# Text rows projected once per table row and spread by one-hot products, in an early-fusion block on one core

## The reference, cut to what matters

```python
# x: (32, 96, 96, 3) images, x_txt: (32, 32) tokens; D = 256, H = 512, S = 16
h = einsum(patchify(x), W_proj) + b_proj + pos_emb           # 36 image rows per sample
t = take(weights, positions(x_txt))                          # 32 text rows per sample
h = concatenate([h, t], axis=1)                              # 68 rows x 32 samples
xn = layernorm(h)
u = xn @ W_x.T + b_x
g = sigmoid(xn @ W_g.T + b_g)
u = u * g + depthwise_conv3(u) * (1 - g)
dt = clip(softplus(xn @ W_dt.T + b_dt).mean(axis=(0, 1)), 0.001, 2.0)   # one per hidden unit
y = ssm_scan(u, exp(A * dt), ...)                            # A = -softplus(A_raw)
h = h + layernorm(xn + y @ W_out.T + b_out)
h = h + moe_top2_of_4(layernorm(h))
```

## Time and profile before

| | us |
|---|---|
| runs (3) | 497.41, 498.78, 499.92 |
| median | 498.78 |
| span of the profiled execution | 495.2 |
| median less span | 3.6 |
| PE busy in the span | 442.5 (89%) |
| DVE busy | 330.5 (67%) |
| ACT busy | 296.4 (60%) |

### The profile page before, as it was taken

One profiled execution on the slowest core, in us unless ns is written; L12 is line 12 of the kernel. 1 busy time (PEld: TensorE's weight loads), 2 busy tenths in 40 slices (PEclk: granted clock), 3 DMA queues, 4 the chain that ended last, 5 costly groups with the idle time before them and its releaser, 6 DMA issues.

```text
span 495.2 us, 9980 instructions
## 1 busy us (share of the span) xinstructions
PE 442.5 (89%) x3149; PEld 363.4 (73%) x3149; DVE 330.5 (67%) x980; ACT 296.4 (60%) x667; POOL 152.2 (31%) x255
## 2 busy tenths in 40 slices
PE   8989989799899999999999798999999999999400
PEld 5769967667778878887777577888878888888300
DVE  6885567678999434335786777866674666666584
ACT  2854359177975465316554354887786777877341
POOL 2000000000000000001243887874778644543322
PEclk9999999799999999999999999999999999999955
DMA  7981089900019942972511222232322333252262
GB/s 178 187 228 56 33 253 322 292 0 2 1 35 259 217 114 58 228 228 81 180 54 52 89 94 77 86 97 66 107 98 76 107 107 110 74 155 69 78 213 82
DMA packets 58734, 59.94 MB, mean 121 GB/s; under 512 B 25368, under 2 KB 51260, under 8 KB 57404
## 3 DMA queue, kind: packets, MB, share of 16 engines
q1 hardware_dynamic: 54236, 48.68, 36.4%
q0 software_dynamic: 3552, 9.74, 5.3%
q10 hardware_dynamic: 896, 0.89, 0.6%
HBM read 34.50 MB, written 24.80 MB: 120 GB/s over the span
## 4 chain that ended last, share of the span: by engine, by line
PE 66%; DVE 12%; issue 7%; ACT 7%; POOL 4%; DMA 2%; SPq 1%; DVEq 0%; POOLq 0%; ACTq 0%
PE bank L1040 14%; PE bank L881 9%; PE bank L433 8%; PE bank L435 8%; PE bank L434 8%; PE bank L955 3%; PE bank L1030 3%; PE bank L901 3%; POOL sorted_x L671 2%; PE bank L1012 2%; ACT U L470 1%; DVE spj L1400 1%; DMA got<-expert_y 1%; PE bank L848 1%; PE bank L947 1%
## 5 line engine op out<-in xcount | busy, mean ns | idle before, releaser
L1040 PE MATMUL bank<-w,hr 128*128 x320 | 76.0, 380 | 1.5 <-DVE ysb L1661 1.5
L1040 PEld LDWEIGHTS bank<-w,hr 128*128 128x128 f32 x320 | 60.1, 190 | 11.7 <-issue 2.7
L644 POOL MEMSET ones<- 2x128 f32 x1 | 0.2, 194 | 212.3 <-PE bank L916 212.3
L1234 ACT ACTIVATE hr<-bank,gsel 128x128 f32<-128x128 f32 x160 | 59.9, 460 | 0.2 <-PE bank L1030 0.2
L719 POOL DMA_INDIRECT expert_y<-ysb,toid x40 | 42.8, 1071 | 51.3 <-DVE ysb L1661 34.7
L881 PE MATMUL bank<-Tb,U 68*32 68x68 f32 x1024 | 45.9, 358 | 0.3 <-issue 0.3
L881 PEld LDWEIGHTS bank<-Tb,U 68*32 68x32 f32 x1024 | 40.6, 139 | 3.6 <-issue 3.1
L1646 DVE BATCH_NORM_STATS2 bsth<-bank 128x6 f32<-128x512 f32 x40 | 27.7, 693 | 20.5 <-PE bank L435 20.2
L671 POOL DMA_INDIRECT sorted_x<-x2s,slot x34 | 33.8, 994 | 15.3 <-issue 9.2
L1226 ACT ACTIVATE hn<-bank,nmrh,rsh 128x512 f32<-128x512 f32 x40 | 31.1, 777 | 10.0 <-DVE nmrh L1655 8.1
L433 PE MATMUL bank<-w_hi,bT_hi 128*128 x80 | 35.0, 438 | 0.1
(11 more groups left out here) (297 smaller groups left out, 1153.3 us busy)
## 6 DMA issues: line engine op xcount, KB each, us to landing
Tb<-ssm_kernels SPq DMA_DIRECT2D x16, 680.0 KB, 7.5
sorted_x<-zpad SPq DMA_DIRECT2D x6, 1419.0 KB, 13.6
xg<-sorted_x SPq DMA_DIRECT2D x40, 129.0 KB, 2.1
got<-expert_y SPq DMA_DIRECT2D x17, 256.0 KB, 3.6
XI<-in_x_dram SPq DMA_DIRECT2D x12, 288.0 KB, 5.6
h0r<-h_spill SPq DMA_DIRECT2D x17, 128.0 KB, 2.1
out_dram<-acc SPq DMA_DIRECT2D x17, 128.0 KB
w1raw<-in_L_ffn_w_dram SPq DMA_DIRECT2D x4, 512.0 KB, 15.9
```

Source lines behind the costliest of these rows:

```text
L1040: mm = pe.matmul(bank[6][:, 0:D], hr[:, i % 3, c, :], w2[:, bass.ds(expert[i], 1), c, :].rearrange("p o n -> p (o n)"), start=(c == 0), st ...
L1234: last = act.activation(hr[:, i % 3, c, :], bank[3 + i % 2][:, c * P:(c + 1) * P], ACT.Relu, scale=gsel[:, i, 0, c:c + 1], bias=gsel[:, i, ...
```

## The change

Text tiles are no longer normalised, transposed and projected one by one. The table's 34 rows are normalised in place (`mvt`, `sdt`, `tn`); their reciprocal deviation and shift are carried as two further columns of the table, so that a1 spreads them with the rows and the spill holds them (258 columns, `DX`). The ring has five new entries: a count of each table row's use (`cnt`), the transposed normalised table (`tx`), its time step (`dtt`), and its projections by W_x and W_g (`pt`). Text blocks of `project` become two matmuls with the one-hot rows. The time step's text part is softplus over 34 columns, multiplied by the counts and summed. The blocks are now three of 384 image columns and two of 512 text columns; the time-step sweep goes over the image blocks alone, 12 quarters. Steps a2 to a4 are made for image tiles only, and image tiles keep their places in the list.

```diff
-    BLOCKS = [(n, min(512, N - n)) for n in range(0, N, 512)]
+    NI = LI * B
+    BLOCKS = [(n, NI // 3) for n in range(0, NI, NI // 3)] + [(n, 512) for n in range(NI, N, 512)]
+    NBI = 3
     NB = len(BLOCKS)
+    VT = LT + 2
...
-        BLOCK_ORDER = [3, 4, 0, 1, 2]
...
-        PREP = [("pos", 0), ("pos", 1), ("vec",)] + [("wp", c) for c in range(0, CK, 2)]
+            return (BLOCKS[nb][0] + BLOCKS[nb][1]) // P
+
+        PREP = [("pos", 0), ("pos", 1), ("vec",)] + [("wp", c) for c in range(0, CK, 2)] + [("cnt",), ("tx",)]
         IMAGES = [("img", half, g, wp) for g in range(2) for wp in range(HP) for half in range(2)]
         WEIGHTS = [("w", w, dc) for w in range(3) for dc in range(DC)]
-        A_RING = PREP + IMAGES + WEIGHTS
-        LAST_IMAGES = (len(PREP) + len(IMAGES) - 2, len(PREP) + len(IMAGES) - 1)
-
+        TEXTS = [("dtt",), ("pt", 1), ("pt", 2)]
+        A_RING = PREP + IMAGES + WEIGHTS + TEXTS
         A_STEPS = [("ring", q) for q in range(len(PREP))]
         ahead = list(range(len(PREP), len(A_RING)))
         for k in range(NT + 3):
-            A_STEPS += [(f"a{s + 1}", TILE_ORDER[k - s]) for s in (3, 2, 1, 0) if 0 <= k - s < NT]
+            A_STEPS += [(f"a{s + 1}", TILE_ORDER[k - s]) for s in (3, 2, 1, 0)
+                        if 0 <= k - s < NT and (s == 0 or k - s >= NH0)]
...
+                wide = DX if n == 0 else D
...
-                    pe.wait_ge(sem("xT"), NT)
+                    pe.wait_ge(sem("xT"), NTI)
...
-                    if kind == "vec":
+                    if kind == "cnt":
+                        pe.wait_ge(sem("text_dve"), 3)
+                        mm = pe.matmul(ps[:, 0:VT], cntw[:], ident[0:VT, 0:VT], start=True, stop=True)
+                    elif kind == "tx":
+                        pe.wait_ge(sem("text_dve"), 2)
+                        for dc in range(DC):
+                            mm = pe.transpose(ps[:, dc * VT:(dc + 1) * VT], tn[:, dc * P:(dc + 1) * P], ident[0:VT, 0:VT])
+                    elif kind == "dtt":
+                        pe.wait_ge(sem("a_read"), A_RING.index(("w", 0, DC - 1)) + 1)
+                        for j in range(HC):
+                            for dc in range(DC):
+                                mm = split3(pe, ps[:, j * VT:(j + 1) * VT], WT[0][0][:, dc, j * P:(j + 1) * P],
+                                            WT[0][1][:, dc, j * P:(j + 1) * P], xTt_hi[:, dc, :], xTt_lo[:, dc, :],
+                                            dc == 0, dc == DC - 1)
+                    elif kind == "pt":
+                        w = rest[0]
+                        pe.wait_ge(sem("a_read"), A_RING.index(("w", w, DC - 1)) + 1)
+                        for dc in range(DC):
+                            mm = split3(pe, ps[0:VT, :], xTt_hi[:, dc, :], xTt_lo[:, dc, :], WT[w][0][:, dc, :],
+                                        WT[w][1][:, dc, :], dc == 0, dc == DC - 1)
+                    elif kind == "vec":
...
-                    m = TILE_ORDER.index(step[1])
+                    m = step[1]
...
+                    if nb >= NBI:
+                        ps, at_n = bank[first + c % 2][:, 0:w], OH[:, n0 - NI:n0 - NI + w]
+                        pe.matmul(ps, PT[wt][0][:, j * P:(j + 1) * P], at_n, start=True, stop=False)
+                        pe.matmul(ps, PT[wt][1][:, j * P:(j + 1) * P], at_n, start=False, stop=True).then_inc(sem(done), 1)
+                        continue
...
             pe.wait_ge(sem("a_read"), len(A_RING))
+            pe.wait_ge(sem("xT"), NTI)
             for nb in range(NB):
-                pe.wait_ge(sem("xT"), ready_tiles(nb))
                 project(0, nb)
 
             def idle(ps, count):
@@ -849,7 +886,7 @@
 
             pe.wait_ge(sem("v_init"), 4)
             idle(bank[1], 20)
-            for q in range(AHEAD, HC * NB):
+            for q in range(AHEAD, HC * NBI):
...
+            act.wait_ge(sem("text_dve"), 1)
+            act.wait_ge(sem("consts"), 6)
+            act.activation(sdt[:], mvt[:, 1:2], ACT.Sqrt, bias=epsc[0:VT, :]).then_inc(sem("text_act"), 1)
             act.preload_act_table_set("natural_log_exp_and_others")
             act.wait_ge(sem("a_capped"), 1)
             act.activation(atmp[:], atmp[:], ACT.Exp).then_inc(sem("a_exp"), 1)
             act.wait_ge(sem("a_exp"), 1)
-            act.wait_ge(sem("consts"), 6)
...
+                    elif kind == "tx":
+                        act.wait_ge(sem("a_ps"), q + 1)
+                        copy(xTt_hi[:].rearrange("p c v -> p (c v)"), ps[:, 0:DC * VT]).then_inc(sem("text_act"), 1)
+                    elif kind == "pt":
+                        act.wait_ge(sem("a_ps"), q + 1)
+                        copy(PT[rest[0]][0][:], ps[0:VT, :]).then_inc(sem("text_act"), 1)
...
+                if first == 0:
+                    act.wait_ge(sem("text_dve"), 4)
+                    act.activation(zs[:], zs[:], ACT.Exp).then_inc(sem("text_act"), 1)
+                    act.wait_ge(sem("text_act"), 5)
+                    act.activation(zs[:], zs[:], ACT.Ln, bias=onec[:]).then_inc(sem("text_act"), 1)
...
+            dve.wait_ge(sem("table_in"), 16)
+            link(dve.bn_stats(bstt[:], tabl[:, 0:D]))
+            signal(dve.bn_aggr(mvt[:], bstt[:]), "text_dve", 1)
...
-            dve.wait_ge(sem("table_in"), 16)
+            dve.wait_ge(sem("text_act"), 1)
+            link(dve.reciprocal(tabl[:, D:D + 1], sdt[:]))
+            mark(dve.scalar_tensor_tensor(tabl[:, D + 1:D + 2], mvt[:, 0:1], -1.0, tabl[:, D:D + 1], ALU.mult, ALU.mult))
+            dve.tensor_scalar(tn[:], tabl[:, 0:D], mvt[:, 0:1], tabl[:, D:D + 1], ALU.subtract, ALU.mult).then_inc(
+                sem("text_dve"), 1)
+            need(linked[0])
...
+                        if k == 1:
+                            link(dve.reduce_sum(cnt[:], OH[:].bitcast(F32), AX))
+                            dve.tensor_copy(cntw[:], cnt[:].broadcast_to([VT, P])).then_inc(sem("text_dve"), 1)
+                    elif kind == "cnt":
+                        dve.tensor_copy(cnt_b[:], ps[:, 0:VT]).then_inc(sem("a_read"), 1)
+                    elif kind == "tx":
+                        dve.wait_ge(sem("text_act"), 2)
+                        dve.tensor_tensor(xTt_lo[:].rearrange("p c v -> p (c v)"), ps[:, 0:DC * VT],
+                                          xTt_hi[:].rearrange("p c v -> p (c v)").bitcast(F32), ALU.subtract
+                                          ).then_inc(sem("a_read"), 1)
+                    elif kind == "dtt":
+                        for j in range(HC):
+                            mark(dve.tensor_scalar(zt[:, j, :], ps[:, j * VT:(j + 1) * VT], vec[:, bdt0 + j:bdt0 + j + 1],
+                                                   None, ALU.add))
+                        need(linked[0])
+                        dve.sem_inc(sem("a_read"), 1)
+                        dve.tensor_scalar(zs[:], zt[:], 40.0, None, ALU.min).then_inc(sem("text_dve"), 1)
+                    elif kind == "pt":
+                        w = rest[0]
+                        dve.wait_ge(sem("text_act"), w + 2)
+                        dve.tensor_tensor(PT[w][1][:], ps[0:VT, :], PT[w][0][:].bitcast(F32), ALU.subtract
+                                          ).then_inc(sem("a_read"), 1)
...
+            dve.wait_ge(sem("text_act"), 6)
+            link(dve.tensor_tensor(zt[:], zt[:], zs[:], ALU.max))
+            link(dve.tensor_tensor(zt[:], zt[:], cnt_b[:].rearrange("p (o v) -> p o v", o=1).broadcast_to([P, HC, VT]),
+                                   ALU.mult))
+            link(dve.reduce_sum(dts[:, :, NBI], zt[:], AX))
+            dve.wait_ge(sem("dt_read"), HC * NBI)
             link(dve.reduce_sum(dt1[:], dts[:], AX))
```

More of the change, by code:

```diff
@@ L125, in build_kernel @@
         onec = sb("onec", [P, 1])
-        dts = sb("dts", [P, HC, NB])
+        dts = sb("dts", [P, HC, NBI + 1])
+        bstt = sb("bstt", [VT, 6])
+        mvt = sb("mvt", [VT, 2])
+        sdt = sb("sdt", [VT, 1])
+        cnt = sb("cnt", [VT, 1])
         dt1 = sb("dt1", [P, HC])
@@ L452, in lo_chunk @@
         def lo_chunk(c):
-            return pT_lo[0][:, c, 0:LI * B] if c < KT else pT_lo1[:, c - KT].rearrange("p t b -> p (t b)")
+            return pT_lo[0][:, c, :] if c < KT else pT_lo1[:, c - KT].rearrange("p t b -> p (t b)")
         def patches_lo(half, g, wp):
-            a = pT_lo[0][:, 0:KT, 0:LI * B] if half == 0 else pT_lo1[:].rearrange("p c t b -> p c (t b)")
+            a = pT_lo[0][:] if half == 0 else pT_lo1[:].rearrange("p c t b -> p c (t b)")
             return a.rearrange("p c (hp wp b) -> p c hp wp b", hp=HP, wp=HP)[:, :, :, wp, g * GB:(g + 1) * GB]
@@ L664, in _ @@
                     pool.wait_ge(sem("small_in"), 80)
-                    pool.tensor_tensor(h0r[:, i % 4, :], h0r[:, i % 4, :], lnb_b[:], ALU.add).then_inc(sem("h0b"), 1)
+                    pool.tensor_tensor(h0r[:, i % 4, 0:D], h0r[:, i % 4, 0:D], lnb_b[:], ALU.add).then_inc(sem("h0b"), 1)
```

(33 more changed lines are left out.)

75 lines of the change are left out of this document (39 added, 36 removed).

## The result

| | before | after |
|---|---|---|
| median, us (four runs each) | 498.10 | 507.11 |
| lowest to highest | 497.25 to 499.92 | 504.75 to 508.21 |
| span of the profiled execution | 495.2 | 504.7 |

After over before is 1.018, 95% interval [1.014, 1.022]: slower, where 483.8 was forecast and 477.0 to 491.5 was the range.

A forecast was written before the change was run, and what follows sets the result against it. Limits differ by stage: TensorE in the tiles and scan, VectorE in the loop and after the sum. 1.2 + 4.8 - 1.5 - 13.1 - 2.1 - 4.3 = -15.0 us: span 480.2, time 483.8, range 477 to 491.5.

The forecast's parts named there:

- Step 1: Head and image loop: later start, 3.9 us TensorE idle, 1.0 us for the clock; +1.2 us, bounds -1.3 and +4.
- rival C: Head's gap puts TensorE at 1.2 GHz, image loop doesn't restore it: 500.8 us, 504 with one tile; chance 0.04, plus 0.01.
- Step 2: Image tile stage, TensorE full: 24 short matmuls 2.7 us, table projections 2.7, text transposes leaving 0.7; together +4.8 us.
- Step 3: First four quarters of the time step: shorter TensorE quarters and ScalarE passes; -1.5 us.
- Step 4: From 75.4 us to the sum over time steps: fewer quarters, 1.3 us for the clock's return; -13.1, within 2 us.
- Step 5: From the sum to the first scan product: cheaper projections, limited by the first fetch landing at 151 us; -2.1 us.
- Step 6: Scan stage: one more cheaper row of projections between scans on a full TensorE; -4.3 us.
- Rival A: Projections' gain after the sum and in the scan hidden by waits for fetch and ScalarE: 490.2 us; chance 0.14.
- rival D: Text rows no cheaper, products over 34 table rows slower per column than over 128: +7, time 491 us; chance 0.02.

The follow-up runs named there:

- run 1: The changed kernel with 16 filler matmuls (results unused) on TensorE in the head's wait, ahead of the second pair of patch-weight transposes: 489.34 us.
- run 11: The changed kernel, head's wait unfilled, with two fillers of 512 columns ahead of each image piece in place of one: 492.69 us.
- run 3: The changed kernel, head's wait left in, with a burst of 24 fillers of 512 columns at the loop's first image piece: 494.80 us.
- run 2: The kernel before the change with four extra copies on VectorE ahead of the table's split, so that TensorE waits in the head: 511.06 us.
- run 7: As run 5, with the count moved into the image loop, 7 fillers among the first mixed-row transposes and 5 before the first scan product: 480.29 us.
- run 9: As run 1, with 6 fillers in the head's wait in place of 16: 489.09 us.
- run 10: As run 1, with 2 fillers in the head's wait in place of 16: two executions, 509.35 and 489.30 us.
- run 4: The changed kernel reordered: one-hot rows before the table's normalisation, image positions split within the loop, `cnt` and `tx` behind the weights: 487.16 us.
- run 5: As run 4, plus 18 fillers on TensorE ahead of the ninth quarter of the time step: 485.34 us.

## Why the prediction was wrong, step by step

**Step 1, the head, is the step that failed**, and in it only the term for the clock. The start was right: 16.4 us forecast, 16.94 measured. The wait was right: 3.9 us forecast, 3.44 measured. The fall was expected as well. Its price was put at 1.0 us, after the gap at 95.33, behind which the clock soon came back. Measured: the loop takes 32.0 us where it takes 18.5 at full clock (run 1), 13.5 us; 1.1 more go before it (it starts at 15.8 in run 1) and 3.2 in the tiles, 17.8 in all. The argument against rival C was that the clock "came back under work like this". But the work behind 95.33 was matmuls of 512 moving columns, and the loop's is mostly transposes of 96 columns, three to a filler. With that work TensorE counts as busy for 96% of 32 us and the clock stays down (after); with 24 more fillers it comes back after one step (run 11). The engine's occupation said nothing of its clock.

That the loop's work is why the clock stayed down is shown by runs 3 and 11; why such work doesn't bring it back stays open.

Rival C named the fall, its place and its deciding point. Its reason was another: it had the loop's steps wait on VectorE and ScalarE, and they hardly wait. It gave 500.8 us for the loop alone and 504 with one tile; 507.1 came, so its size was nearly right (it doubled the steps, they grew 1.8 times), in part because the scan stage lost what the sum had gained. Its chance of 0.04 was far too small.

The Trainium skill, page "TensorE: Matmul & The Clock Gate", section "Part 1: The HAM clock gate", has the low clock as the default and activity as what lifts it. The 0.50 of the loop's row is that low level, but TensorE's occupation of 96% didn't lift it. The Trainium skill's section "Part 4: PE-mode transpose", on the same page, goes further: full clock doesn't engage for transposes made in the transpose mode. The prediction overlooked that sentence. The profile lists these transposes as matmuls and doesn't show their mode. The loops of the changed kernel and of run 2 fit the sentence for a start at 1.2 GHz, for 32 and for 24.9 us; but in run 2 the clock then came back within the loop, and the same loop begun at 2.4 GHz kept it (run 1, and the kernel before).

**Step 2, the tiles**: +4.8 forecast (its terms add up to 4.7); +5.6 at full clock (runs 1 and 11, 39.7 us against 34.1), +8.8 in the changed kernel. The 24 short matmuls took 0.1125 us each (73.27 to 75.97), 2.7 in all, as the row for 128 columns had it. By the Trainium skill's 60 cycles, section "Back-to-back issue gap" of the same page, the estimate was 0.6; here the measurement decides. That they can be followed by a stretch at 1.2 GHz (run 7) the prediction didn't have.

**Step 3** can't be told apart from its neighbours by the marks.

**Step 4**: -13.1 forecast, -13.7 measured, with the expected wait (5.20 us) and four quarters at the low clock. With that wait filled it was -14.5 (run 7), inside the bound given.

**Step 5**: -2.1 forecast, -2.0 measured, and TensorE waits for the first fetch, as forecast. The closeness is partly luck: the step's own figures (1.1 at 152.2, 4.3 at 149, landing at 151) give 2.3, the clock was at 0.89 in this stretch, and run 7 gained 1.3.

**Step 6**: -4.3 forecast, +1.6 measured, -4.7 in run 7. The gain was there and was given back: 4.0 us in waits that end in nothing the profile shows, and the remaining 1.9 beside a clock of 0.93. Why those waits arise stays open. Rival A (ScalarE and the fetches hide the gain) didn't happen in this step, since run 7 has it all. Nor did rival D: the products over 34 table rows start 0.23 us apart in run 1 (84.51, 84.74, 84.97), as those over 128 rows do. The argument brought against it compared how long single products last (0.38 us at 256 columns, 0.39 at 512), which says nothing on their price in a row.

With most of the clock kept, the rest of the sum holds within 2 us. Without the head's term it was -16.2 us, and -17.5 without the 1.3 for the clock in step 4. In run 7's profiled execution the span falls by 19.9, of which 4.3 stand at the first image tile (29.9 instead of 34.2 us) through the new order of the head, and 15.6 behind it. Its four runs' median is 3.2 us above that execution.

A smaller slip: of the 3.6 us taken to lie around the span, 1.7 do in every execution; the rest was the distance of the profiled execution from the median.

## What to carry to other kernels

Before a change lengthens a wait of TensorE, look at the work that follows it. If that work is narrow (small transposes, few moving columns), price the wait not by itself but by the whole stage behind it at 1.2 GHz, until rows show otherwise, and give that case a large share of the chances. Filling the wait with useless matmuls is a one-line test, and here it was the cure; better is an order of the head in which the wait doesn't arise. Run 7, with that order and with fillers at later waits, was 27 us faster than the change as made.

## What the runs showed of the hardware that was not expected

- TensorE can count as busy for 31 of 32 us and run at 1.2 GHz all that time.
- A wait of 1.92 us in the head was not followed by a fall (run 9); waits of 2.13 (run 10), 2.86 (run 3), 3.38 (run 2) and 3.44 us were. With 2 fillers the same kernel gave 509.35 and 489.30 us on one chip; the slower had the wait of 2.13 us, the faster wasn't profiled. This kernel has two times, 20 us apart.
- The clock can fall with no wait before it: behind 24 matmuls of 34 columns, with TensorE occupied for all of the 2.6 us, 3.4 us at 1.2 GHz followed (run 7).
- Once the first long fall is gone, the shorter ones are worth less: four covers took the changed kernel from 487.2 (run 4) to 480.3 us, 1.8 of it by the first of them (run 5).
- TensorE had a wait of 1.9 to 3.3 us within the scan in six of the thirteen profiled executions, with nothing in the profile that ends them, in kernels with and without the change.
